# Cross attention with the keys on the partitions, two heads at a time: values before scores on TensorE, subtraction before maximum on VectorE

## What is computed

```python
hidden_states = jnp.concatenate([context, latents], axis=1)      # 4096 + 256 = 4352 rows
q = (latents @ Wq).reshape(b, q_len, N_KV_HEADS, N_GROUPS, HEAD_DIM)   # 32 heads of 128, in 4 groups of 8
k = (hidden_states @ Wk).reshape(b, kv_len, N_KV_HEADS, HEAD_DIM)
v = (hidden_states @ Wv).reshape(b, kv_len, N_KV_HEADS, HEAD_DIM)
scores = jnp.einsum('bqhgd,bkhd->bhgqk', q, k) * scale
attn = jax.nn.softmax(scores.astype(jnp.float32), axis=-1).astype(q.dtype)
out = jnp.einsum('bhgqk,bkhd->bqhgd', attn, v)
return out.reshape(b, q_len, N_HEADS * HEAD_DIM) @ Wo
```

## Time and profile before

| | |
|---|---|
| median of three runs | 2156.7 us (2156.37 to 2159.44) |
| the profiled execution | 2159.04 us |
| its span, first to last instruction | 2157.2 us |
| mean granted TensorE clock | 0.994 of full |
| keys and values, until TensorE's last matmul of it | 383.3 us |
| cross attention, until the first matmul with `wo` | 1519.6 us |
| TensorE busy | 98% of the span |
| VectorE, ScalarE, GpSimd busy | 58%, 50%, 9% |

### The profile page before, as it was taken

The page is one execution under the profiler, slowest core; times in us unless marked ns, Lnnn a source line. Parts: engine busy times, 40 slices in busy tenths (PEclk is TensorE's granted clock), DMA queues, the critical chain, the costliest instruction groups (busy, mean ns, idle before and its releaser), DMA issues. The chain is left out here.

```text
span 2157.2 us, 38230 instructions
## 1 busy us (share of the span) xinstructions
PE 2111.0 (98%) x14054; PEld 1937.6 (90%) x14054; DVE 1247.2 (58%) x2591; ACT 1070.2 (50%) x1604; POOL 192.2 (9%) x98
## 2 busy tenths in 40 slices
PE   8999999999999999999999999999999999999998
PEld 6888888799998999998999899998779999999886
DVE  5211110567676767766676767676574566666555
ACT  4111111566566656575666666566444544455442
POOL 0000001300012100031000310000000000000110
PEclk9999999999999999999999999999999999999999
DMA  6222212200012000120000210001745444455362
GB/s 234 102 113 97 78 69 80 82 26 13 24 45 78 14 26 12 46 75 27 14 25 30 76 41 13 26 12 55 274 148 209 181 175 175 179 189 191 133 233 79
DMA packets 57385, 199.28 MB, mean 92 GB/s; under 512 B 4592, under 2 KB 22000, under 8 KB 51760
## 3 DMA queue, kind: packets, MB, share of 16 engines
q1 hardware_dynamic: 57264, 197.71, 25.7%
HBM read 170.43 MB, written 27.26 MB: 92 GB/s over the span
## 5 line engine op out<-in xcount | busy, mean ns | idle before, releaser
L747 DVE TENSOR_TENSOR xa_pT_lo<-xa_t_ps,xa_pT_hi 128x512 fp32r<-128x512 f32 x544 | 372.6, 690 | 334.9 <-ACT xa_pT_hi L626 334.7
L626 ACT ACTIVATE xa_pT_hi<-xa_t_ps 128x512 fp32r<-128x512 f32 x544 | 321.8, 597 | 411.9 <-PE xa_t_ps L822 400.9
L105 PE MATMUL xa_o_ps<-xa_pT_hi,xa_v_hi 128*128 128x256 f32 x1088 | 310.1, 285 | 2.2 <-DVE xa_pT_lo L747 2.1
L107 PE MATMUL xa_o_ps<-xa_pT_hi,xa_v_lo 128*128 128x256 f32 x1088 | 308.5, 284 | 0.0
L106 PE MATMUL xa_o_ps<-xa_pT_lo,xa_v_hi 128*128 128x256 f32 x1088 | 307.9, 283 | 0.0
L822 PE MATMUL xa_t_ps<-ident,xa_rows 128*128 128x128 f32 x1632 | 294.8, 273 | 2.9 <-DVE xa_pT_lo L747 2.9
L722 DVE TENSOR_SCALAR_CACHE_REDUCE xa_rows<-xa_s_ps 128x512 f32<-128x512 f32 (+1 forms) x432 | 274.7, 652 | 0.2 <-PE xa_s_ps L107 0.2
L105 PE MATMUL xa_s_ps<-split,xa_qT_hi 128*128 128x512 f32 (+1 forms) x576 | 250.9, 436 | 0.9 <-DVE xa_qT_lo L716 0.9
L620 ACT ACTIVATE xa_rows<-xa_rows,xa_neg_max 128x1088 f32<-128x1088 f32 x192 | 229.6, 1196 | 0.0
L105 PEld LDWEIGHTS xa_o_ps<-xa_pT_hi,xa_v_hi 128*128 128x128 f32 x1088 | 207.2, 190 | 16.8 <-DVE xa_pT_lo L747 3.4
L107 PE MATMUL xa_s_ps<-split,xa_qT_lo 128*128 128x512 f32 (+1 forms) x576 | 220.8, 383 | 0.0
(11 more groups left out here) (287 smaller groups left out, 4744.8 us busy)
## 6 DMA issues: line engine op xcount, KB each, us to landing
pair_raw<-in_w_qk SPq DMA_DIRECT2D x15, 2048.0 KB, 8.3
pair_raw<-in_w_gv SPq DMA_DIRECT2D x15, 2048.0 KB, 8.3
full<-in_wo SPq DMA_DIRECT2D x16, 1024.0 KB, 5.2
pair_raw<-in_w_out SPq DMA_DIRECT2D x16, 1024.0 KB, 5.1
xa_w_raw<-in_wq SPq DMA_DIRECT2D x31, 512.0 KB, 3.7
full<-in_ctxT SPq DMA_DIRECT2D x7, 2048.0 KB, 8.3
stage<-v_scratch SPq DMA_DIRECT2D x16, 544.0 KB, 3.8
kT_scratch<-kv_k_out SPq DMA_DIRECT2D x8, 1024.0 KB, 4.1
```

The lines of the kernel that those rows point to most:

```text
L105: pe.matmul(out, w_hi, m_hi, start=first, stop=False)
L107: return pe.matmul(out, w_lo, m_hi, start=False, stop=last)
L626: act.activation(pT_hi[j % NPT][:, :, :], t_ps[:, (par * PAIRS + j) % 2, :, :], ACT.Copy).then_inc(pT_hi_ready, 1)
L747: dve.tensor_tensor(pT_lo[j % NPT][:, :, :], t_ps[:, (par * PAIRS + j) % 2, :, :], f32(pT_hi[j % NPT][:, :, :]), ALU.subtract).then_inc(pT ...
```

## The change

It rewrites the cross attention; the other stages keep their work, apart from how keys are stored.

- A pass handles a pair of heads of one key-value head. Scores come with the keys on the partitions: for a block of 128 keys, `three_pass` with the key block as weights and the two heads' queries as 512 moving columns. A step j has two such blocks (6 matmuls), 17 steps a pair, 16 pairs.
- Nothing is turned. The maximum over the keys is taken across blocks by VectorE in `peak` (L742 to L755), at the end of the pair by 4 transposes and a reduction; a matmul of ones with a diagonal matrix of the maxima (`diag`, made by ScalarE) puts them on every partition in `r_ps`.
- ScalarE copies the scores of a step out of PSUM (`act_row`); in the next pair's time VectorE subtracts `r_ps` from them (`dve_shift`, L765) and ScalarE takes the exponential into one of three `probs` tiles. GpSimd adds the `probs` of a pair up (L688), and a matmul with ones spreads the sums.
- The product with the values is one matmul in plain float32, 128x512 moving, in place of three in fp32r: `v` and `probs` aren't split.
- In step j VectorE does the subtraction of block j + 1 before the maximum of block j; TensorE does the values of block j before the scores of block j + 1. After the last step TensorE makes the 4 transposes, three quarters of the query after next (`FILL` = 12 of 16 triples), the spreading matmul, and the rest of that query.
- The reciprocal of the sums is taken on 128x512 of PSUM in four parts, in steps 4 to 7. GpSimd multiplies it with the output.
- The last pair has no scores beside it. Its sums are added by GpSimd (odd blocks) and VectorE (even blocks); then come four matmuls, four reciprocals and a product.
- `project_keys_values` stores the keys already split (high by ScalarE, low by VectorE, two DMAs for each of four groups a chunk), so that no engine splits them later; the values stay whole.

The core of the diff; line numbers in the text from L742 up are those of the new kernel where they name its helpers.

```diff
+PAIRS = HEADS // 2
+W = 2 * TOK
+J = KVT // 2
+ENDS = (4, 8, 12, J)
...
         def copy_keys(act, c, n):
             for g in range(KVH):
                 act.wait_ge(k_ready, KVH * c + g + 1)
-                act.activation(k_out[:, g, 0:n], k_ps[:, g, 0:n], ACT.Copy).then_inc(k_copied, 1)
+                act.wait_ge(k_stored[g % 2], 64 * c + 32 * (g // 2) + 32)
+                act.activation(k_hi[:, g % 2, 0:n], k_ps[:, g, 0:n], ACT.Copy).then_inc(k_hi_ready, 1)
...
+        def copy_low_keys(dve, c, n):
+                dve.tensor_tensor(k_lo[:, g % 2, 0:n], k_ps[:, g, 0:n], f32(k_hi[:, g % 2, 0:n]),
+                                  ALU.subtract).then_inc(k_copied, 1)
...
+FILL = 12
+KEEP = 3
...
+        def act_row(act, n, b, j, first=False):
+            act.wait_ge(peak_done, J * n + j + 1)
+            if not first:
+                act.wait_ge(exp_done, J * (n - 1) + j + 1)
+            act.activation(rows[j], s_ps[:, 2 * b:2 * b + 2, :], ACT.Copy).then_inc(row_ready, 1)
...
+            act.activation(probs[j % KEEP], rows[j], ACT.Exp, scale=SCALE).then_inc(exp_done, 1)
...
+                pool.wait_ge(added, (J - 1) * n + j - 1)
+                pool.tensor_tensor(sums[:, :, :], sums[:, :, :], probs[j % KEEP], ALU.add).then_inc(added, 1)
...
+        def dve_slot(dve, n, u, g, first=False, last=False):
+            has_prev, has_next, has_query = flags(u, first, last)
+            for j in range(J):
+                if j + 1 < J:
+                    dve_shift(dve, n, j + 1)
                 if has_next:
+                    dve_peak(dve, n + 1, (u + 1 + j) % 2, j)
...
+                if has_prev and 4 <= j < 8:
+                    dve_inverse(dve, n - 1, j - 4)
...
+        def pe_scores(pe, n, par, b, j, keys, first=False):
...
+            if not first or j >= 2:
+                pe.wait_ge(row_ready, J * n + j - 1)
...
+        def pe_values(pe, n, j, values, first):
...
+            pe.wait_ge(exp_done, J * n + j + 1)
             for t in range(2):
                 at = slice((2 * j + t) * P, (2 * j + t + 1) * P)
+                last = pe.matmul(o_ps[:, :], v[:, at], probs[j % KEEP][:, t, :], start=j == 0 and t == 0,
+                                 stop=j == J - 1 and t == 1)
...
+        def pe_slot(pe, n, u, g, first=False, last=False):
...
+            if has_next:
+                pe_scores(pe, n + 1, 1 - par, (u + 1) % 2, 0, keys)
+            for j in range(J):
+                pe_values(pe, n, j, values, not has_prev)
+                if has_next and j + 1 < J:
+                    pe_scores(pe, n + 1, 1 - par, (u + j) % 2, j + 1, keys)
+                if has_prev and j == 2:
+                    pe_sums(pe, n - 1)
+            if has_next:
+                pe_peak(pe, n + 1)
+                if has_query:
+                    pe_query(pe, n + 3, 0, FILL)
+                pe_spread(pe, n + 1)
+                if has_query:
+                    pe_query(pe, n + 3, FILL, 2 * KT)
```

More of the change, by code:

```diff
@@ L253, in _ @@
         def _(sp):
-            sp.sem_inc(k_stored, 16)
+            for par in range(2):
+                sp.sem_inc(k_stored[par], 32)
             sp.sem_inc(v_stored, 16)
@@ new lines, in flags, with load_weight, load_keys @@
+        def flags(u, first, last):
+            return not first, not (last and u == 3), not last
+        def load_weight(sp, m):
+            sp.wait_ge(w_lo_ready, m - 1)
+            sp.dma_start(w_raw[:, :, :], wq[bass.ds(m, 1)].rearrange("h p k d -> p (h k) d")).then_inc(w_in, 16)
+        def load_keys(sp, g, i):
+            at = piece_columns(i)
+            for region, dram in zip(shared.r, k_drams):
+                sp.dma_start(f32(region[:, at]), dram[bass.ds(g, 1)].rearrange("g p n -> (g p) n")[:, at]).then_inc(k_in[i], 16)
@@ L571, in sync_slot @@
                     proj.load(sp, step, step)
-            store_o(sp, n, u % 2)
+            for i, end in enumerate(ENDS):
+                if i == 2 and has_prev:
+                    store_o(sp, n - 1, 1 - u % 2)
+                if not last and u == 2:
+                    sp.wait_ge(s_done, J * (n + 1) + end)
+                    load_keys(sp, g + 1, i)
+                if not last and u == 3:
+                    sp.wait_ge(pv_done, J * n + end)
+                    load_values(sp, g + 1, i)
@@ new lines, in act_exp @@
+        def act_exp(act, n, j, first=False, last=False):
+            act.wait_ge(shifted, J * n + j + 1)
+            back = j - KEEP
+            if back >= 0:
+                act.wait_ge(pv_done, J * n + back + 1)
+                if not last:
+                    act.wait_ge(added, (J - 1) * n + max(back, 1))
+                elif back >= 2 and back % 2 == 0:
+                    act.wait_ge(added_last, back // 2)
+                else:
+                    act.wait_ge(added, (J - 1) * n + (back + 2) // 2)
+            elif not first:
+                before = max(x for x in range(J) if x % KEEP == j)
+                act.wait_ge(pv_done, J * (n - 1) + before + 1)
+                act.wait_ge(added, (J - 1) * (n - 1) + before)
+            act.activation(probs[j % KEEP], rows[j], ACT.Exp, scale=SCALE).then_inc(exp_done, 1)
@@ new lines, in pe_scores, with pe_peak, pe_spread @@
+            last.then_inc(s_done, 1)
+        def pe_peak(pe, n, first=False):
+            pe.wait_ge(peak_done, J * (n + 1))
+            if not first:
+                pe.wait_ge(inverse_ready, 4 * n)
+            for b in range(W // P):
+                at = slice(b * P, (b + 1) * P)
+                last = pe.transpose(t_ps[:, at], peak[:, 0, at], ident[:, :])
+            last.then_inc(peak_turned, 1)
+        def pe_spread(pe, n, first=False):
+            pe.wait_ge(diag_ready, (W // P) * (n + 1))
+            if not first:
+                pe.wait_ge(shifted, J * n)
+            pe.matmul(r_ps[:, :], ones[:, :], diag[:, :], start=True, stop=True).then_inc(spread, 1)
@@ new lines, in pe_sums, with pe_sums_last @@
+        def pe_sums(pe, n):
+            pe.wait_ge(sum_ready, n + 1)
+            pe.wait_ge(max_ready, n + 2)
+            pe.matmul(t_ps[:, :], ones[:, :], sum_row[:, :], start=True, stop=True).then_inc(sum_spread, 1)
+        def pe_sums_last(pe):
+            pe.wait_ge(inverse_ready, 4 * LAST + 4)
+            pe.wait_ge(added, (J - 1) * LAST + J // 2)
+            pe.wait_ge(added_last, J // 2)
+            pieces = [part[:, t, :] for part in (sums, peak) for t in range(2)]
+            for i, part in enumerate(pieces):
+                last = pe.matmul(t_ps[:, :], ones[:, :], part, start=i == 0, stop=i == len(pieces) - 1)
+            last.then_inc(sum_spread, 1)
```

739 lines of the change are left out of this document (338 added, 401 removed).

## The result

The changed kernel takes **2045.44 us** (median of 4 runs, 2043.84 to 2048.79), the kernel before on the same chip 2156.53: ratio **0.948, 95% interval 0.947 to 0.950**. The prediction was 2057, range 2030 to 2112. The profiled execution is the one of 2043.84 us, its span 2042.0.

What follows compares the result with a forecast made beforehand. TensorE, 98% busy, was taken as the bound. Terms from 383.3 to `wo` summed to 1034.3 against 1136.3 us: minus 102, plus 1.7, so minus 100; forecast 2057 us for a median of 2156.7, range 2030 to 2112.

Steps and rivals of the forecast that it cites:

- to the first scores: Cross attention entry: 2 us wait, doubled first query of 5.8, half clock 1.7, query split 1.5; 11.2 us after 383.3.
- opening: First 17 score steps without values beside them, second query included, 40 us; then maxima, query and spread, 8.7.
- last pair's values: Last pair, values alone: VectorE and GpSimd additions one after the other, 4.0 us for two steps, 34 in all.
- exit: After the last values: four float32 matmuls 3.5, reciprocals 5.7, product 0.7, block change 1.9; 11.8 us.
- The unknown price: TensorE's plain float32 matmul of 512 columns, in no earlier trace: 0.872 us, two records at the transposes' rate.
- Rival 3: Value matmuls: weight loads in the open, 1.25 us a float32 matmul, 206 us more, 2263 us; chance 0.06.
- rival 4: Value matmuls: cheap float32 at 0.454 us, VectorE binds at about 54 a pair, about 1930 us; chance 0.02.
- rival 1: Value matmuls: float32 costs four fp32r matmuls, 0.908 us, 20 us more, 2077 us; chance 0.20.
- TensorE's stream: TensorE's work for a pair of heads: scores 23.2, values 29.6, query 5.8 and small terms, 60.7 us against 69.3.
- 1.6 us of stall a pair: Steady pairs: 0.9 us from VectorE's reciprocals in steps 4 to 7, the rest at the pair's end; 62.3 a pair.
- Pairs 13 and 14: No query left to cover the spread maxima chain: 3.5 us more stall each, 59.8 us a pair.
- Rival 2: Steps: late values, first on TensorE, block scores; 3.4 us a pair more than booked, 2101 us; chance 0.17.

Runs made afterwards that it cites:

- experiment 6: Changed kernel with GpSimd's additions to the sums cut to 8 columns, all but the first of a pair: 2044.88 us.
- Experiment 10: Changed kernel with ScalarE splitting the second query weight before the first scores and GpSimd taking VectorE's part of the first `wo` split: 2039.55 us.
- experiment 2: Changed kernel with TensorE making the scores of block j + 1 before the values of block j: 2045.87 us.
- experiment 8: Changed kernel with one more 128x512 maximum on VectorE in 13 of the 17 steps: 2069.38 us.
- experiment 1: Changed kernel with VectorE taking the maximum of block j before the subtraction of block j + 1: 2162.51 us.
- experiment 3: Changed kernel with both orders turned: maximum before subtraction on VectorE, scores before values on TensorE: 2126.96 us.
- experiment 4: Changed kernel with maximum before subtraction on VectorE, scores before values on TensorE, and ScalarE's score copy before its exponential: 2044.78 us.
- 5: Changed kernel with maximum before subtraction on VectorE and ScalarE's score copy before its exponential, TensorE's order kept: 2164.19 us.

## Why the prediction was right, and where its terms were off

The mechanism held: the transposes leave TensorE's stream, the float32 price is the one taken from them, and the other engines hide behind the rest. The size of the gain was 14.6 us too small in the stage, and that is a net figure: three terms were too long by 24.0 us together, two too short by 9.4, so that the measured time lies nearer to the forecast than the terms do. That part is luck.

The sum, from the end of keys and values to the start of `wo`, in us of the profiled execution:

| term | predicted | measured |
|---|---|---|
| to the first scores | 11.2 | 9.2 |
| opening: 17 score blocks, query, spread | 48.7 | 53.7 |
| the 15 pairs with scores | 928.6 | 909.8 |
| last pair's values | 34 | 38.4 |
| exit | 11.8 | 8.6 |
| sum | 1034.3 | 1019.7 |
| the rest of the program | +1.7 | +2.4 |

- **The unknown price** held: 0.872 from the transposes, 0.870 measured. Rival 3 (loads in the open, 1.25) and rival 4 (0.454) fall far off with this one row, rival 1 (four fp32r matmuls, 0.908) by 0.038, 20 us on the whole. The Trainium skill's rule of four passes (FP8 and Floating Point Precision, TensorE Precision Notes) fits the time: four times the 0.213 us of rival 1 for 512 columns at 2.4 GHz are, as an estimate, 0.853 us. The trace shows two records a matmul and 0.870 us, not 0.908, which speaks against four passes that each pay the 14 ns of rival 1.
- **TensorE's stream**, 60.7 a pair, held: ten pairs take 60.69 to 60.71.
- **The step that was off: 1.6 us of stall a pair.** It was two terms. Reciprocals of 128 columns cost 0.947 us and not 1.43, so the line from one column more does not carry from 2 to 128, and the deficit of steps 4 to 7 stays inside the lead. And L749 did meet GpSimd, 0.70 to 2.90 us, median 1.14, but nothing on TensorE waited for it: experiment 6 takes most of GpSimd's work away and gains nothing there. 12 pairs of 1.6 and 0.7 in the first are 19.9 us, against 18.8 in the table's third row, which also holds 2.5 us at the two turns of the loop that the sum had at nothing.
- **Pairs 13 and 14**: the stalls came where I had them, for `diag` and for the first probabilities, but shorter: 3.3 us at one end and 4.65 at the other, where I had 1.6 + 3.5 = 5.1. By the starts of L867 both pairs take 58.6 us and not 59.8 (my terms add up to 60.0; to the first scores they add up to 11.0, not 11.2).
- **To the first scores**, 2.0 us too long: 1.7 of it was half clock as in the earlier trace rows, and the granted clock was 1.00 there.
- **The opening** was 5 us too short: I had 7 us for the second query, 5.8 of them its matmuls. Its wait for GpSimd's split alone was 4.67, and the granted clock was 0.5 from 404.4 to 411.2. Experiment 10 shows both.
- **The last pair**: I had VectorE and GpSimd slow each other in their additions, and they did not (VectorE's took 1.21 to 1.23). What came instead is what the sum had at nothing: half clock over the first records, 2.6 us, and the first `wo` split, which VectorE does in mid-pair (the two halves of L975 take 4.5 us, one of them stretched by GpSimd). Experiment 10 gives 2.5 back; its first eight records still take 6.48 us.
- **The exit** was 3.2 us too long: 2.3 of it the reciprocals (3.4 and not 5.7), 1.0 the change of block (0.9 and not 1.9).
- **Rival 2** (values block scores) did not come; experiment 2 shows that TensorE's order is free here. VectorE's deficit at the reciprocals shows only when it gets more work (experiment 8), 1.3 us a pair. Late values do hold up the scores in experiment 1, 7.5 us a pair, but by the order, with VectorE busy 69%. The prediction used the lead as a half sentence; it is the condition on which the 111 us stand.
- **Keys and values**, booked at nothing: their end moved from 383.3 to 382.3.
- **Signs** named for the forecast that did not come: a pair of 62 us, waits at the peak transposes, reciprocals near 1.4 us.

## What to carry to other kernels

When several engines pass blocks along a loop, write down for each engine what stands ahead of the instruction that the next one waits for, and compare that chain, hand-overs included, with the cover that the bound engine gives; here the order of two instructions on an engine that is busy 69 to 75% of the steady stretch was worth the change's whole gain. Change one order and the rows ahead of it on the following engines have to be read again: experiment 3 failed in ScalarE's order, though only VectorE's and TensorE's had been touched. Where the path to the probabilities is short of cover, one more step of lead gave all of the loss back (experiment 4 against 5); a faster instruction was not tried. An instruction that another engine stretches costs nothing as long as there is lead (L749 in experiment 6) and stands in the chain ahead of a wait when there is none (L749 in experiment 3).

## What the hardware showed that was not expected

- A float32 matmul is two records of 0.435 us for 512 columns, each nearly twice an fp32r matmul (0.227); that makes it a little cheaper than four of those (0.908), and dearer than three (0.681). Removing 136 transposes for two heads paid for it.
- A reciprocal of 128x128 from PSUM takes 0.947 us on VectorE (64 of them, 0.894 to 0.958), while 128x2 takes 0.166.
- A VectorE instruction with two SBUF operands beside a GpSimd one: 0.695 us undisturbed, up to 2.90 (L749, 16 of them); 1.22 and 3.36 for a split of 128x1024 (L975). VectorE's seven additions of the last pair, of the same kind, kept 1.21 to 1.23: none began well inside one of GpSimd's.
- The granted clock fell to half around stops of TensorE: 404.4 to 411.2 with a wait of 4.67 us, 1353.3 to 1360.1 with waits of 2.09 and 2.56. A float32 record of 512 columns starts 0.85 us after the one before there, against 0.435.
